# Second attention of a two-layer transformer on one core: the nine banks of max scores of a group in another order

## The chip, the cores and the metric

The kernel is one program on one core of a Trainium2 chip. The metric is the device time of one execution in microseconds (us). Five engines work side by side, each through its own list of instructions in order: PE (TensorE, matmuls; its weight loads are shown apart as PEld), DVE (VectorE), ACT (ScalarE), POOL (GpSimd) and SP (SyncE, which starts transfers). They wait for each other by semaphores.

## What is computed

Two layers: a linear attention and a mixture of experts, then a second attention with softmax and another mixture of experts. The change lies in the second attention alone. Cut to that:

```python
qkv = x @ Wqkv                                   # four sequences of 512, 32 query heads, 8 key heads
scores = jnp.einsum('bhqd,bhkd->bhqk', q, k) / math.sqrt(HD)
scores = jnp.where(causal, scores, -jnp.inf)
aw = jax.nn.softmax(scores, axis=-1)             # max over the keys, exp, sum
aw = aw[:, :, 0] - lam * aw[:, :, 1]
attn = jnp.einsum('bhqk,bhkd->bhqd', aw, v) * (1.0 - LAMBDA_INIT)
```

## The kernel before

The second attention (`phase_last`) runs over 32 groups (`GROUPS`), one for each sequence and key head. A group has 512 keys in four blocks of 128, and the queries of its four heads, 2048 rows in all, in 16 **granules** of 128 rows.

The softmax needs the maximum of each row before the exponential. So the scores are computed twice. The first time, `max_scores(g, a)` on PE (L1981 to L1998) computes the scores granule by granule; granule t has 32 x (t + 1) columns of keys, since the causal mask cuts the rest, so they run from 32 to 512 columns. The granules are packed into nine PSUM **banks** of at most 512 columns by the table `MAX_GRANULES` (L1219); entry a of the table says which granules are in bank a, and the physical bank is a modulo 3. On DVE, `maximum(g, a)` (L1709 to L1721) waits for the bank, adds the mask and reduces each granule of it to one column of `neg_max` (two rows in the trace for each: the reduction and the reading of its accumulator). Before PE may fill a bank again, DVE must be done with the bank three places earlier (`max_done`, L1990).

The second time, `scores(g, e)` (L2000) makes two matmuls of 512 columns for each of five steps e, a **score pair**, into two of four PSUM banks in turn; the maxima ride along as extra rows of the weights' operand. ACT takes the exponential of a pair in one instruction (`exponentials`, L1862 to L1869). Pair e may be written when the exponential of the pair two earlier is done. POOL cuts off the masked corner of the blocks on the diagonal, and `values(g, kb)` (L2013) multiplies the probabilities of key block kb with the values; its matmuls use a quarter of the array each.

The order on PE is written out by hand in the loop over the groups (L2122 on): while the scores of group g run, the maxima of group g + 3 (`LEAD`) are put between them, by `rows(...)`:

```python
scores(g, 0); rows(0); scores(g, 1); rows(1)
values(g - 1, 1), values(g - 1, 2), values(g - 1, 3)
rows(2); scores(g, 2); rows(3, 4); scores(g, 3); rows(5)
values(g, 0); rows(6); scores(g, 4); rows(7, 8)
```

`rows(n)` is place n of the table. This full pattern holds for groups 1 to 28. The maxima of groups 0 and 1 come before the loop, mixed with the last query, key and value products, those of groups 2 and 3 in group 0, two places for each call of `rows`, with short matmuls without use between them (`warming`). On DVE, `maximum` runs over all groups and places in the same order; in groups 0 and 1 the remainders of the queries (`remainders`, L1637), on which query products and later parts wait, come after the first four places. POOL splits the finished maxima of a group into three parts (`split_maxima`), and a transfer brings them to the place from which `scores` reads them, two groups later.

Of the kernel before, what the change touches and what calls it, by code (L numbers as in the profile page):

```python
# [1215 lines left out]
MASKED = -3.0e38  # L1216


MAX_GRANULES = [(15,), (14,), (13,), (12,), (11, 3), (10, 4), (9, 5), (8, 6), (7, 2, 1, 0)]  # L1219

SLOTS = [(kb, tq) for kb in range(NQ) for tq in range(kb, NQ)]
FIRST = [SLOTS.index((kb, kb)) for kb in range(NQ)]
NA, NE = len(MAX_GRANULES), len(SLOTS) // 2
NORM_AT = 2
# [5 lines left out]
def phase_last(nc, dram, sb, ps):  # L1230
# [3 lines left out]
    with ExitStack() as ctx:  # L1234
# [391 lines left out]
        def _(ve):  # L1626
# [82 lines left out]
            def maximum(g, a):  # L1709
# [4 lines left out]
                off = 0  # L1714
                for n, t in enumerate(MAX_GRANULES[a]):
                    width = 32 * (t + 1)
# [223 lines left out]
        def _(pe):  # L1940
# [40 lines left out]
            def max_scores(g, a):  # L1981
# [10 lines left out]
                off = 0  # L1992
                for t in MAX_GRANULES[a]:
                    width = 32 * (t + 1)
# [316 lines left out]
```

How the kernel before makes its waits and increments, by code:

```python
    def wait(self):  # L39
        self.eng.wait_ge(self.sem, self.base + self.n)
# [71 lines left out]
    def deviations(self, gp, b):  # L112
        gp.wait_ge(self.var_ready, b + 1)
        self.nc.gpsimd.tensor_tensor(self.rstd[:, b * NI:(b + 1) * NI], self.veps[:, b * NI:(b + 1) * NI],
                                     self.minus_half[:, 0:NI], ALU.pow).then_inc(self.rstd_ready, 1)
# [1 line left out]
    def lines(self, ve, b):  # L117
        ve.wait_ge(self.rstd_ready, b + 1)
        self.nc.vector.scalar_tensor_tensor(self.line[:, b * NI:(b + 1) * NI], self.mv[:, b * NI:(b + 1) * NI, 0], -1.0,
                                            self.rstd[:, b * NI:(b + 1) * NI], ALU.mult, ALU.mult).then_inc(self.line_ready, 1)
# [1 line left out]
    def normalise(self, ac, b):  # L122
        ac.wait_ge(self.line_ready, b + 1)
        for t in range(b * NI, (b + 1) * NI):
            last = self.nc.scalar.activation(self.xn[:, t, :], self.x[:, t, :], ACT.Identity, scale=self.rstd[:, t:t + 1],
                                             bias=self.line[:, t:t + 1])
        last.then_inc(self.xn_ready, 1)
# [74 lines left out]
    def choose(self, ve, ch, half):  # L202
# [1 line left out]
        def wide(ap):
            return ap.unsqueeze(2).to_broadcast([P, HALF, E])
        falling = self.sb["falling"][:].unsqueeze(1).to_broadcast([P, HALF, E])
        ve.wait_ge(self.logits_mm, 2 * half + 2)
        logits = self.ps[:, self.logits_bank[2 * half], 0:HALF * E].rearrange("p (t e) -> p t e", e=E)
        ch.link(nc.vector.tensor_reduce(self.top[:, t], logits, AX.X, ALU.max))
```

## Time and profile before

| | us |
|---|---|
| median of 3 runs | 586.7 |
| the runs | 586.08, 586.70, 589.87 |
| span of the profiled execution | 586.0 |
| PE matmul busy | 526.7 (90%) |
| PE weight load busy | 374.2 (64%) |
| DVE busy | 424.8 (72%) |
| ACT busy | 328.6 (56%) |
| POOL busy | 315.5 (54%) |

The span runs from the first to the last instruction of one profiled execution; its own time is about that of the fastest run, 586.08. Busy shares are means over stages with different limits: the stretch that this document speaks of reaches from about 165 us (the first max scores) to about 400 us (the last). All times in the rows are in microseconds from the span's start. PEclk is TensorE's granted clock as a share of 2.4 GHz. Matmuls are pipelined, so the ends of PE's rows are modelled and overlap with the next row's start; starts are what is compared.

### The profile page before, as it was taken

To read this page: it belongs to the slowest core of one execution; us is meant where nothing else is said; L and a number is where in the kernel's file an instruction comes from. 1 tells how busy PE (TensorE), PEld (TensorE's weight loads), DVE (VectorE), ACT (ScalarE), POOL (GpSimd) and SP (SyncE) were. 2 spreads that over 40 slices of the span, in tenths; PEclk is the share of its full clock that TensorE was granted. 3 is DMA by queue.
4 is the path that set the end of the run, shared out by engine and by line. 5 is a ranking of instruction groups with operands and counts; after the bars stand their busy time and mean duration, and the time that the engine had idled before them with its cause. 6 is when DMAs were issued, how large, how long until landed. Compare 5 with 4: busy or idle time off the path is not lost.

```text
span 586.0 us, 13132 instructions
## 1 busy us (share of the span) xinstructions
PE 526.7 (90%) x4044; PEld 374.2 (64%) x4044; DVE 424.8 (72%) x1662; ACT 328.6 (56%) x544; POOL 315.5 (54%) x478
## 2 busy tenths in 40 slices
PE   5989979967489999999999999999998899999960
PEld 5667769965157445444444454445577799999960
DVE  4776736735859899999999999996678454454436
ACT  3854426632573477777777777776630544444423
POOL 3441154417644486566686668666710677777630
PEclk9999989998699899999999999999999899999995
DMA  8500112221671546647634653433850111111115
GB/s 317 221 2 19 55 35 71 71 70 52 126 145 24 122 104 129 126 108 169 153 88 110 154 135 72 93 91 66 299 151 19 45 48 51 49 49 51 43 37 204
DMA packets 90498, 58.21 MB, mean 99 GB/s; under 512 B 72674, under 2 KB 76771, under 8 KB 88615
## 3 DMA queue, kind: packets, MB, share of 16 engines
q1 hardware_dynamic: 81550, 41.18, 28.0%
q0 software_dynamic: 3744, 7.68, 5.1%
q10 hardware_dynamic: 5136, 8.52, 4.1%
q8 instruction: 35, 0.57, 0.4%
q14 instruction: 33, 0.26, 0.2%
HBM read 37.72 MB, written 19.63 MB: 98 GB/s over the span
## 4 chain that ended last, share of the span: by engine, by line
PE 76%; DVE 12%; DMA 4%; issue 3%; ACT 3%; POOL 2%; SPq 0%; ACTq 0%; POOLq 0%; DVEq 0%
PE banks L1167 15%; PE banks L2021 13%; PE banks L2009 12%; PE banks L1995 11%; PE banks L1180 9%; DVE banks L1718 2%; PE banks L1961 1%; PE banks L1154 1%; PE banks L765 1%; DMA f_hg<-scratch_h_rows,r_source 1%; PE banks L366 1%; DMA a_at<-scratch_back_rows,home 1%; PE banks L2109 1%; DVE f_upd L1080 1%; DVE a_rest_ L1637 1%
## 5 line engine op out<-in xcount | busy, mean ns | idle before, releaser
L1718 DVE CUSTOM_DVE_ANT_1 banks<-banks,a_mask 128x480 f32<-128x480 f32 (+14 forms) x480 | 190.0, 459 | 14.7 <-PE banks L1995 12.9
L1867 ACT ACTIVATE a_prob_<-banks 128x1024 f32<-128x1024 f32 x160 | 154.1, 1021 | 48.7 <-PE banks L2009 48.7
L1534 POOL TENSOR_SCALAR_AFFINE_SELECT a_prob_<-a_prob_ 128x512 f32<-128x512 f32 x128 | 80.8, 635 | 67.0 <-ACT a_prob_ L1867 67.0
L1995 PEld LDWEIGHTS banks<-a_k_u_,a_q_u_ 72*128 72x128 bf16 x512 | 64.9, 148 | 64.5 <-DVE a_neg_max_ L1718 31.1
L1995 PE MATMUL banks<-a_k_u_,a_q_u_ 72*128 72x512 bf16 (+15 forms) x512 | 102.4, 291 | 2.4 <-DVE a_neg_max_ L1718 2.4
L1167 PE MATMUL banks<-f_hgt,f_w_now 128*112 128x128 f32 (+1 forms) x808 | 101.2, 277 | 0.0
L2009 PE MATMUL banks<-a_q_u_,a_k_x_ 75*128 75x512 bf16 x320 | 97.4, 386 | 0.4 <-ACT a_prob_ L1867 0.4
L1167 PEld LDWEIGHTS banks<-f_hgt,f_w_now 128*112 128x112 f32 (+1 forms) x808 | 95.6, 184 | 0.0
L978 POOL DMA_INDIRECT f_hg<-scratch_h_rows,r_source x62 | 59.6, 962 | 61.2 <-DVE r_source L299 31.6
L2021 PE MATMUL banks<-a_prob_,a_v_g_ 128*32 128x512 f32 (+3 forms) x1024 | 83.5, 444 | 0.4 <-POOL a_prob_ L1534 0.4
L1718 DVE DVE_READ_ACCUMULATOR2_ANT a_neg_max_<- 128x1 f32 x512 | 72.3, 143 | 0.0
L1180 PE MATMUL banks<-w,f_hidt 112*128 (+1 forms) x496 | 66.2, 277 | 0.0
L1180 PEld LDWEIGHTS banks<-w,f_hidt 112*128 112x128 f32 (+1 forms) x496 | 60.9, 193 | 0.4 <-issue 0.4
L1111 ACT COPY f_w_now<-w 128x448 f32 (+1 forms) x62 | 31.3, 506 | 41.8 <-issue 22.4
L984 POOL DMA_INDIRECT scratch_back_rows<-f_y,r_home x39 | 38.4, 984 | 27.3 <-DVE f_y L1056 26.9
L1042 DVE TENSOR_TENSOR f_hidt<-banks,f_sil 112x512 f32<-112x512 f32 x39 | 27.0, 692 | 33.6 <-PE banks L1167 28.0
L2021 PEld LDWEIGHTS banks<-a_prob_,a_v_g_ 128*32 128x32 f32 x1024 | 27.1, 110 | 37.0 <-issue 19.7
L1030 DVE COPY f_w_now<-w 128x448 f32 (+1 forms) x62 | 25.9, 418 | 30.7 <-issue 29.7
L1095 ACT COPY f_hgt<-banks 128x128 f32<-128x128 f32 x62 | 16.4, 265 | 52.2 <-PE banks L1154 52.2
L2009 PEld LDWEIGHTS banks<-a_q_u_,a_k_x_ 75*128 75x128 bf16 x320 | 26.6, 102 | 17.0 <-ACT a_prob_ L1867 12.5
L1512 POOL TENSOR_SCALAR a_k_x_<-a_k_u_ 72x512 bf16<-72x512 bf16 x32 | 35.4, 1105 | 0.1
L1878 ACT COPY a_o_sb_<-banks 128x512 f32<-128x512 f32 x32 | 18.7, 585 | 18.7 <-PE banks L2021 18.7
(247 smaller groups left out, 714.1 us busy)
## 6 DMA issues: line engine op xcount, KB each, us to landing
a_q_u_<-scratch_q_parts SPq DMA_DIRECT2D x15, 576.0 KB
scratch_o_rows<-a_o_sb_ ACTq DMA_DIRECT2D x28, 256.0 KB, 2.2
w<-in_w SPq DMA_DIRECT2D x2, 2048.0 KB, 10.5
w<-in_w SPq DMA_DIRECT2D x2, 1792.0 KB, 12.3
scratch_q_parts<-a_part_ SPq DMA_DIRECT2D x24, 128.0 KB
a_k_u_<-scratch_k_parts SPq DMA_DIRECT2D x48, 48.0 KB
f_back<-scratch_back_rows SPq DMA_DIRECT2D x4, 512.0 KB, 4.7
w<-in_w SPq DMA_DIRECT2D x2, 896.0 KB, 19.6
```

The source lines that it names most:

```text
L978: nc.gpsimd.indirect_dma_start(out=hg[s % AHEAD][:], out_offset=None, in_=h_rows[:, :], in_offset=bass.IndirectOffsetOnAxis(ap=source[:, s ...
L984: nc.gpsimd.indirect_dma_start(out=back_rows[:, :], out_offset=bass.IndirectOffsetOnAxis(ap=home[:, s:s + 1], axis=0), in_=y[s % YR][:], i ...
L1111: nc.scalar.copy(w_now[s % 2][:, 0, :], w_first(e)).then_inc(w_a, 1)
L1167: last = nc.tensor.matmul(PS[0:FC, 4 + 2 * q + n, c * P:(c + 1) * P], w_now[q][:, n, c * FC:(c + 1) * FC], hgt[q][:], start=True, stop=True)
L1180: last = nc.tensor.matmul(PS[:, 2 + q, 0:D], hidt[q][0:FC, c, :], w_down[0:FC, bass.ds(e, 1), c, :].rearrange("p a d -> p (a d)"), start=( ...
L1512: nc.gpsimd.tensor_scalar(k_x[g % RING][0:ROWS, :].rearrange("r (t c) -> r t c", c=CK), k_u[r][:, :, g % 2 * TG:(g % 2 + 1) * TG].rearrang ...
L1534: nc.gpsimd.affine_select(out=block_p, in_=block_p, pattern=[[0, JH], [1, P]], compare_op=ALU.is_ge, fill=0.0, base=0, channel_multiplier= ...
L1718: last = nc.vector.tensor_tensor_reduce(out=found, in0=found, in1=mask[:, :, TG - 4 * (t + 1):], scale=-1.0, scalar=-MASKED, op0=ALU.add, ...
L1867: nc.scalar.activation(prob[g % 2][:, 2 * e:2 * e + 2].rearrange("p s j t c -> p (s j) t c"), PS[:, b0:b0 + 2, :].rearrange("p s (j c t) - ...
L1995: last = nc.tensor.matmul(PS[:, a % 3, off:off + width], queries[:, g % 2, :, t], k_u[r][:, :, g % 2 * TG:g % 2 * TG + 4 * (t + 1)], start ...
L2009: last = nc.tensor.matmul(PS[:, 3 + 2 * ((NE * g + e) % 2) + n, :], k_x[g % RING][0:ROWS + PARTS, kb * P:(kb + 1) * P], queries[:, g % 2, ...
L2021: last = nc.tensor.matmul(PS[32 * j:32 * (j + 1), 7, kb * P:].rearrange("p (q f) -> p q f", f=P), v_g[g % VR][:, kb, :], prob[g % 2][:, FI ...
```

## The change

One line, the table that packs the granules into banks. The nine banks hold the same granules as before; the order in which they come is another. The bank of four small granules (256, 96, 64 and 32 columns, 448 in all; called the small bank below) moves from the last place to the first, the one of 384 and 128 columns to the second, and the others follow in a new order.

```diff
-MAX_GRANULES = [(15,), (14,), (13,), (12,), (11, 3), (10, 4), (9, 5), (8, 6), (7, 2, 1, 0)]
+MAX_GRANULES = [(7, 2, 1, 0), (11, 3), (15,), (14,), (8, 6), (9, 5), (13,), (12,), (10, 4)]
```

In columns, the places hold 512, 480, 448, 416, 512, 512, 512, 512, 448 before, and 448, 512, 512, 480, 512, 512, 448, 416, 512 after.

PE, in the loop, from the fifth score pair of a group to the first values of the next (L2009 are score pairs, L1995 max scores, L2021 values; `a_k_u`, `a_q_u` and `a_k_x` are keys and queries). Before:

```order
L2009 MATMUL banks<-a_q_u1_,a_k_x2_ 128x512 x2
L1995 MATMUL banks<-a_k_u2_,a_q_u2_ 128x288
L1995 MATMUL banks<-a_k_u2_,a_q_u2_ 128x224
L1995 MATMUL banks<-a_k_u2_,a_q_u2_ 128x256
L1995 MATMUL banks<-a_k_u2_,a_q_u2_ 128x96
L1995 MATMUL banks<-a_k_u2_,a_q_u2_ 128x64
L1995 MATMUL banks<-a_k_u2_,a_q_u2_ 128x32
L2009 MATMUL banks<-a_q_u1_,a_k_x3_ 128x512 x2
L1995 MATMUL banks<-a_k_u3_,a_q_u3_ 128x512
L2009 MATMUL banks<-a_q_u1_,a_k_x3_ 128x512 x2
L1995 MATMUL banks<-a_k_u3_,a_q_u3_ 128x480
```

The same place on PE after the change:

```order
L2009 MATMUL banks<-a_q_u1_,a_k_x2_ 128x512 x2
L1995 MATMUL banks<-a_k_u2_,a_q_u2_ 128x416
L1995 MATMUL banks<-a_k_u2_,a_q_u2_ 128x352
L1995 MATMUL banks<-a_k_u2_,a_q_u2_ 128x160
L2009 MATMUL banks<-a_q_u1_,a_k_x3_ 128x512 x2
L1995 MATMUL banks<-a_k_u3_,a_q_u3_ 128x256
L1995 MATMUL banks<-a_k_u3_,a_q_u3_ 128x96
L1995 MATMUL banks<-a_k_u3_,a_q_u3_ 128x64
L1995 MATMUL banks<-a_k_u3_,a_q_u3_ 128x32
L2009 MATMUL banks<-a_q_u1_,a_k_x3_ 128x512 x2
L1995 MATMUL banks<-a_k_u3_,a_q_u3_ 128x384
L1995 MATMUL banks<-a_k_u3_,a_q_u3_ 128x128
```

Between the fifth pair and the second pair of the next group stood 960 and 512 columns; now stand 928 and 448.

PE, from the end of the first value run to the next values, before:

```order
L2021 MATMUL banks<-a_prob0_,a_v_g1_ 32x128 x4
L1995 MATMUL banks<-a_k_u3_,a_q_u3_ 128x448
L2009 MATMUL banks<-a_q_u1_,a_k_x3_ 128x512 x2
L1995 MATMUL banks<-a_k_u3_,a_q_u3_ 128x416
L1995 MATMUL banks<-a_k_u3_,a_q_u3_ 128x384
L1995 MATMUL banks<-a_k_u3_,a_q_u3_ 128x128
L2009 MATMUL banks<-a_q_u1_,a_k_x3_ 128x512 x2
L1995 MATMUL banks<-a_k_u3_,a_q_u3_ 128x352
L1995 MATMUL banks<-a_k_u3_,a_q_u3_ 128x160
L2021 MATMUL banks<-a_prob1_,a_v_g2_ 32x512 x4
```

The same place on PE after the change:

```order
L2021 MATMUL banks<-a_prob0_,a_v_g1_ 32x128 x4
L1995 MATMUL banks<-a_k_u3_,a_q_u3_ 128x512
L2009 MATMUL banks<-a_q_u1_,a_k_x3_ 128x512 x2
L1995 MATMUL banks<-a_k_u3_,a_q_u3_ 128x480
L1995 MATMUL banks<-a_k_u3_,a_q_u3_ 128x288
L1995 MATMUL banks<-a_k_u3_,a_q_u3_ 128x224
L2009 MATMUL banks<-a_q_u1_,a_k_x3_ 128x512 x2
L1995 MATMUL banks<-a_k_u3_,a_q_u3_ 128x320
L1995 MATMUL banks<-a_k_u3_,a_q_u3_ 128x192
L2021 MATMUL banks<-a_prob1_,a_v_g2_ 32x512 x4
```

Directly behind the value run stands the bank of 512 columns instead of that of 448, and the two banks before the fourth pair have 992 columns instead of 928.

## Rows read from the trace of the kernel before

**Rows 1.** Busy time by stretch: us, PE, PEld, DVE, ACT, POOL, clock, DMA share, GB/s.

```profile
269.76:276.83 7.07, 7.07 (x62) 3.51 (x60) 6.72 (x35) 5.39 (x7) 4.97 (x10) 1.00 0.74 181
198.60:202.00 3.40, 3.40 (x27) 1.30 (x27) 1.83 (x11) 1.55 (x3) 2.48 (x6) 0.50 0.10 11
```

**Rows 2.** Who waited for whom, 225 to 390 us: total us, times, longest.

```profile
PEld banks L1995 <- DVE a_neg_max_ L1718: 21.2, 27, 0.8
```

**Rows 3.** PE's timeline of one group: start, us, instructions, [idle before <-releaser].

```profile
270.55 0.63 PE L2009 MATMUL banks<-a_q_u_,a_k_x_ 75*128 75x512 bf16 x2
271.03 0.36 PE L1995 MATMUL banks<-a_k_u_,a_q_u_ 72*128 72x480 bf16 x1
271.32 1.50 PE L2021 MATMUL banks<-a_prob_,a_v_g_ 128*32 128x384 f32 x24
272.76 0.41 PE L1995 MATMUL banks<-a_k_u_,a_q_u_ 72*128 72x448 bf16 x1
273.00 0.62 PE L2009 MATMUL banks<-a_q_u_,a_k_x_ 75*128 75x512 bf16 x2
273.46 0.56 PE L1995 MATMUL banks<-a_k_u_,a_q_u_ 72*128 72x416 bf16 x3
273.86 0.61 PE L2009 MATMUL banks<-a_q_u_,a_k_x_ 75*128 75x512 bf16 x2
274.31 0.38 PE L1995 MATMUL banks<-a_k_u_,a_q_u_ 72*128 72x352 bf16 x2
274.62 1.06 PE L2021 MATMUL banks<-a_prob_,a_v_g_ 128*32 128x512 f32 x8
275.61 0.45 PE L1995 MATMUL banks<-a_k_u_,a_q_u_ 72*128 72x320 bf16 x2
275.89 0.61 PE L2009 MATMUL banks<-a_q_u_,a_k_x_ 75*128 75x512 bf16 x2
276.35 0.64 PE L1995 MATMUL banks<-a_k_u_,a_q_u_ 72*128 72x288 bf16 x6
276.83 0.60 PE L2009 MATMUL banks<-a_q_u_,a_k_x_ 75*128 75x512 bf16 x2
277.27 0.38 PE L1995 MATMUL banks<-a_k_u_,a_q_u_ 72*128 72x512 bf16 x1
277.62 0.63 PE L2009 MATMUL banks<-a_q_u_,a_k_x_ 75*128 75x512 bf16 x2
```

**Rows 4.** The weight loader's timeline: after either value run, and before the second pair.

```profile
272.75 0.14 PEld L1995 LDWEIGHTS banks<-a_k_u_,a_q_u_ 72*128 72x128 bf16 x1 [0.20 <-issue]
...
275.61 0.21 PEld L1995 LDWEIGHTS banks<-a_k_u_,a_q_u_ 72*128 72x128 bf16 x2 [0.84 <-DVE a_neg_max_ L1718]
...
277.62 0.11 PEld L2009 LDWEIGHTS banks<-a_q_u_,a_k_x_ 75*128 75x128 bf16 x2 [0.42 <-ACT a_prob_ L1867]
```

**Rows 5.** The chain of waits: start, us, what (first and last of 26 such).

```profile
218.13 1.00 PE banks L2021 x8
...
394.86 1.00 PE banks L2021 x8
```

**Rows 6.** DVE's timeline: the small bank, the four banks behind it, one steady bank.

```profile
176.89 0.43 DVE L1718 CUSTOM_DVE_ANT_1 banks<-banks,a_mask 128x256 f32<-128x256 f32 x1 [1.42 <-PE banks L1995]
...
177.74 0.77 DVE L1718 CUSTOM_DVE_ANT_0 banks<-banks,a_mask 128x512 f32<-128x512 f32 x1
178.43 0.14 DVE L1718 DVE_READ_ACCUMULATOR2_ANT a_neg_max_<- 128x1 f32 x1
...
180.18 1.81 DVE L1637 TENSOR_TENSOR a_rest_<-banks,a_part_ 128x1024 f32<-128x1024 f32 x2
...
273.20 0.63 DVE L1718 CUSTOM_DVE_ANT_1 banks<-banks,a_mask 128x448 f32<-128x448 f32 x1 [0.28 <-PE banks L1995]
```

**Rows 7.** PE's timeline in group 0 and 1: a late bank and the first long value run.

```profile
196.67 0.47 PE L1995 MATMUL banks<-a_k_u_,a_q_u_ 72*128 72x256 bf16 x4 [0.32 <-DVE a_neg_max_ L1718]
...
198.56 2.79 PE L2021 MATMUL banks<-a_prob_,a_v_g_ 128*32 128x384 f32 x24
```

## The prediction

> **What bounds the kernel now.** The change lives in the second attention, so I read that stretch alone: first busy time by stretch, then the waits, then PE's own timeline of one group, and last the weight loader's timeline, to see which of the waits named there are real.
>
> Busy time by stretch shows one group of the steady part, 7.07 us long: PE busy for all of it, DVE for 6.72, ACT for 5.39, POOL for 4.97, at a granted clock of 1.00, which is 2.4 GHz [rows 1]. The chain of waits agrees: the first-block value product (the piece of 1.00 us) comes back from 218.13 to 394.86 us in 25 steps, 7.07 us each, nearly always by way of PE [rows 5]. Two engines are so close to full that the busy shares alone do not say which one sets the pace. The list of waits points at DVE: the weight loader waited for the maxima 27 times, 21.2 us in all [rows 2]. That is the reading to test.
>
> PE's timeline of a group [rows 3], by starts, runs from the second score pair at 270.55: score pair 0.48, bank of 480 columns 0.29, values 1.44, bank of 448 columns 0.24, pair 0.46, two banks with 928 columns 0.40, pair 0.45, bank of 512 columns 0.31, values 0.99, bank of 512 columns 0.28, and then at 275.89 the fifth pair 0.46, two banks with 960 columns 0.48, the next group's first pair 0.44, its first bank 0.35, and at 277.62 the second pair again. I call 270.55 to 275.89 the **rear piece** (5.34 us) and 275.89 to 277.62 the **front piece** (1.73 us). The 928 columns in 0.40 us give 0.43 ns a column. By this, 480 and 512 columns ahead of values carry a surcharge of 0.08 to 0.09 and the 448 and 512 behind values one of 0.05 to 0.06. Those surcharges are the change to and from the value product, not DVE: behind the first value run the weight loader's idle time is put down to "issue", behind the second to DVE (0.84 us), and both matmuls start equally soon [rows 4]. So the 21.2 us of waiting cost PE nothing in this stretch.
>
> One wait is real. The first bank of 512 columns takes 0.35 where 512 columns take 0.22: PE stands for about 0.13, because the weights of the second score pair wait 0.42 us for the exponential [rows 4]. That pair overwrites the two score banks that the fifth pair of the group before filled, and ACT has to read them first. The front piece is therefore set by a loop of score pair, exponential, score pair, whose length of 1.73 us does not depend on the banks of maxima inside it as long as they fit. PE's own work there is 0.46 + 0.48 + 0.44 + 0.22 = 1.60.
>
> **The change part by part.** Nothing is added or removed: 16 matmuls, 16 reductions and 4352 columns a group stay, and so do all the waits in the code. The banks move between the pieces.
>
> Front piece: seventh and eighth place of the table (counted from nought) and the next group's first. Before 960 + 512 columns; after 416 + 512 and the small bank of 448. The 928 columns cost 0.40. The small bank is not timed alone; the six matmuls with 960 columns took 0.48, of which 512 columns are 0.22, so it is 0.26 (bounds: 0.19 if its four matmuls cost only their columns, 0.48 as a whole group of six). PE's work becomes 0.46 + 0.40 + 0.44 + 0.26 = 1.56 (1.49 to 1.78), under 1.73. The piece stays at 1.73: the 0.04 us of work that left is only a longer wait for ACT, 0.17 instead of 0.13.
>
> Rear piece: places 1 to 6. Before 480 + 448 + 416 + 512 + 512 + 512 = 2880 columns; after 512 + 512 + 480 + 512 + 512 + 448 = 2976. The 96 more columns cost 0.04 us. The surcharges stay: one bank stands ahead of each value run and one behind it, as before. The number of matmuls ahead of the values goes from one to two, which costs nothing beyond columns in the rows (416, 384 and 128 follow one another at the plain column rate). So a group takes 7.11 in place of 7.07. The full pattern runs for groups 1 to 28: 28 x 0.041 = **+1.2 us**.
>
> DVE must not come late. A bank may be written when the one three places earlier is reduced. The narrowest place after the change is the sixth bank, which needs the third, now of 512 columns and directly behind the values. Before, a 448-column matmul at 272.76 [rows 3] had its reduction start at 273.20 [rows 6], 0.44 later; 64 more columns make 0.47. The reduction of 512 takes 0.69 (177.74 to 178.43) and its read-out 0.14 [rows 6]: done 1.30 after the third bank's matmul starts. PE comes to the sixth bank after 0.27 (bank) + 0.46 (pair) + 0.43 (992 columns) + 0.45 (pair) = 1.61, and to its weights one matmul of 0.22 sooner, 1.39. A margin of 0.09 on the weights and 0.31 on the matmul: no wait. DVE's own idle time moves: with the small bank and that of 384 and 128 first, it has less to do before the values end and waits longer for the third bank. That costs nothing, since PE does not wait for it.
>
> The stretch that fills the pipeline: groups 0 and 1 put their first four banks ahead of other work on DVE (the remainders of the queries, L1637). Those four took 180.18 − 177.74 = 2.44. After: the small bank 0.85 (176.89 to 177.74), 512 columns 0.69, 480 columns 0.65, and 384 with 128 at 0.69 plus one more granule (the small bank's three extra granules cost 0.85 − 448/512 x 0.69 = 0.25, so 0.08 each) 0.77: 2.96, all from [rows 6]. The remainders come 0.5 us later, but DVE is the bound there, its total is unchanged, and the banks that now follow are smaller by the same amount. Bounds: 0 and +0.5, if what PE starts behind the remainders is not caught up. I take 0, since the first value products behind it, at 198.56 [rows 7], come after all four groups of maxima.
>
> Sum: +1.2 us. The profiled execution's span is 586.0 and the fastest run 586.08, so about 0.1 lies around it: 587.3 by that execution. The median of the runs shown is 0.6 higher, 586.7: **587.9 us**.
>
> **The rivals.** (a) The change does nothing: PE's 0.35 at the first bank is its own cost and not a wait. Then the front piece gives back the 96 columns, 0.04, and the time stays 586.7. Against it: the same 512 columns take 0.22 elsewhere, and the weight loader's row names ACT.
>
> (b) DVE is the bound, faster. Then the 21.2 us of waits are real, and what counts is DVE's idle time of 0.35 a group (7.07 − 6.72). An order that fills it would save up to 28 x 0.35 = 9.8: 576.9. For it: the wait list, and 95% busy. Against it: the equal starts behind the two value runs. The Trainium skill (Perfetto Trace Analysis, Identifying the Most-Contended Engine) holds matmul busy time for a bad measure and asks for the share of weight loading; that is 3.51 of 7.07 here, half, and by this rule DVE would be called the fuller engine. The rows of starts speak against the rule in this stretch, since column time, surcharges and one wait fill the group.
>
> (c) DVE is late, slower. The third bank is ready 1.44 + 0.47 = 1.91 after the values start. If DVE at that start still has the whole last bank of the group before on hand (384-and-128-like, 0.77) and then the two first banks (0.85 + 0.77), it needs 2.39 and comes 0.48 late to the third; that is done 1.78 after its matmul, and PE, there at 1.61, waits 0.17 in each group: 28 x 0.17 = +4.8, with the +1.2 592.7. It decides from a backlog of some 0.6 at the start of the values. For it: DVE is 95% busy. Against it: the two banks just before are now of 416 and 512 columns instead of 512 and the small one, so less is on hand there than today.
>
> (d) The clock. From 198.60 to 202.00 the granted clock was 0.50, 1.2 GHz [rows 1], after PE had waited for DVE (0.32 us at 196.67), and the value run there took 2.79 us where it takes 1.50 [rows 7, 3]: 1.3 us, and some 0.3 for the bank and the pair behind it. PE's waits in the filling stretch move, above all that for DVE behind the remainders, which grows by the 0.5 us. One more such stretch: +1.6, 589.5. None: −1.6, 586.3. The Trainium skill (TensorE: Matmul & The Clock Gate, A second HAM failure mode) tells of short idle times between groups of matmuls that cycle through PSUM banks and bring the clock down. The steady group has such an idle time and a clock of 1.00, so the trace does not bear that out for the steady part.
>
> **How the numbers follow.** Forecast 0.68, (a) 0.12, (b) 0.04, (c) 0.03, (d) one more 0.08, none 0.05. The range leaves out (b) and (c), 0.07, and reaches from the lower clock case to the upper, with the 0.6 us by which runs lie off the median: 586.3 − 0.6 to 589.5 + 0.6, 585.7 to 590.1. It holds the bounds of the fill (+0.5) and of the small bank (at 0.48 the front piece would grow by 0.05 a group, +1.4: 589.3). A measurement of this kernel tells about 1% (5.9 us) from no change; only (b) lies below that and only (c) above: faster 0.04, within 1% 0.93, slower 0.03.
>
> **What would show it.** In the changed kernel's PE timeline a group should take 7.10 to 7.12 us by starts, the front piece 1.73, the rear piece 5.38, and the second score pair's weights should still wait for the exponential, a little longer. DVE should idle some 0.6 us in front of the third bank. The first value products behind the fill should start within 0.5 us of 198.56. A group of 7.07 speaks for (a), one under 7.0 for (b), a wait of PE for DVE at the sixth bank for (c), another count of stretches at 1.2 GHz between 160 and 210 us for (d). The forecast falls if the front piece changes its length with the banks in it.

## The result, and the profile after

The changed kernel takes 591.0 us in the median of 22 runs (586.77 to 595.89), the kernel before 587.13 us beside it (22 runs, 585.78 to 593.07). The ratio is 1.0067 (95% interval 1.0051 to 1.0083): 3.9 us slower, within 1%, but outside the range of 585.7 to 590.1. The forecast was +1.2.

The runs of one kernel lie in groups that go with the mean granted clock of the run; ratios leave out runs more than 1.5% above the fastest of their kernel, medians do not. For the changed kernel:

| mean clock of the run | runs | time, median | range |
|---|---|---|---|
| 0.960 to 0.961 | 2 | 587.7 | 586.8 to 588.6 |
| 0.958 to 0.959 | 13 | 590.6 | 589.8 to 592.1 |
| 0.947 to 0.951 | 7 | 594.6 | 593.3 to 595.9 |

The kernel before has 116 of its 121 runs in the batches below at 0.960 to 0.966. The profiled execution of the changed kernel took 586.77 us, one of the two in the first line, with a span of 584.9. So it shows what the change does at the high clock, and it does not show what makes most runs longer.

PE's timeline after the change, the small bank in the filling stretch and one steady group (start, us, instructions, idle before and releaser in brackets):

```profile
183.85 0.42 PE L1995 MATMUL banks<-a_k_u_,a_q_u_ 72*128 72x256 bf16 x4
184.12 0.47 PE L2035 MATMUL banks<-a_wqk,ident 128*128 128x128 f32 x2
...
269.46 0.62 PE L2009 MATMUL banks<-a_q_u_,a_k_x_ 75*128 75x512 bf16 x2
269.92 0.38 PE L1995 MATMUL banks<-a_k_u_,a_q_u_ 72*128 72x384 bf16 x2
...
273.27 0.38 PE L1995 MATMUL banks<-a_k_u_,a_q_u_ 72*128 72x320 bf16 x2
273.58 1.06 PE L2021 MATMUL banks<-a_prob_,a_v_g_ 128*32 128x512 f32 x8
274.58 0.41 PE L1995 MATMUL banks<-a_k_u_,a_q_u_ 72*128 72x448 bf16 x1
274.82 0.62 PE L2009 MATMUL banks<-a_q_u_,a_k_x_ 75*128 75x512 bf16 x2
275.29 0.56 PE L1995 MATMUL banks<-a_k_u_,a_q_u_ 72*128 72x416 bf16 x3
275.68 0.61 PE L2009 MATMUL banks<-a_q_u_,a_k_x_ 75*128 75x512 bf16 x2
276.13 0.42 PE L1995 MATMUL banks<-a_k_u_,a_q_u_ 72*128 72x256 bf16 x4
276.56 0.62 PE L2009 MATMUL banks<-a_q_u_,a_k_x_ 75*128 75x512 bf16 x2
```

Against [rows 3]: the rear piece runs from 269.46 to 274.82, 5.36 us (5.34 before), the front piece from 274.82 to 276.56, 1.74 us (1.73 before), the group 7.10 (7.07). Over all steady groups the median from group to group is 7.099 against 7.065. The small bank, the last before 276.56, takes 0.43 there; in the filling stretch, at 183.85, the same bank of another group takes 0.27. The difference of 0.16 is a wait inside the front piece. (The rows left out are the first value run, the third to fifth bank and two pairs.)

The list of waits of the steady part, from 225 to 388 us (us in all, times, longest):

```profile
PEld banks L1995 <- DVE a_neg_max_ L1718: 22.6, 39, 0.8
...
DVE banks L1718 <- PE banks L1995: 9.2, 20, 0.5
```

The weight loader still waits some 22 us for the maxima, as in [rows 2], and DVE now idles for a bank, at most 0.5 us at a time. Neither moves a start on PE.

What else changed for PE lies in the filling stretch, in PE's timeline behind the remainders of the queries. After the change:

```profile
179.78 0.59 PE L2035 MATMUL banks<-a_wqk,ident 128*128 128x256 f32 x2
181.89 0.40 PE L1995 MATMUL banks<-a_k_u_,a_q_u_ 72*128 72x416 bf16 x1 [1.51 <-DVE a_neg_max_ L1718]
```

Before, the same wait, ahead of the same place of the table, was 1.27 us long:

```profile
182.82 0.44 PE L1995 MATMUL banks<-a_k_u_,a_q_u_ 72*128 72x288 bf16 x2 [1.27 <-DVE a_neg_max_ L1718]
```

In both executions the clock stayed at 1.00 over it.

### The profile page after: what moved, and what is told of

Its sections match the earlier page's. It is cut to its first block, busy times and chain, and to the rows that moved or that the text cites. A ratio compares the mean times of both kernels' runs of the same rounds, so it can differ in the third digit from the quotient of the medians.

```text
span 584.9 us, 13132 instructions
## 1 busy us (share of the span) xinstructions
PE 526.5 (90%) x4044; PEld 380.1 (65%) x4044; DVE 424.3 (73%) x1662; ACT 328.5 (56%) x544; POOL 316.0 (54%) x478
## 4 chain that ended last, share of the span: by engine, by line
PE 76%; DVE 11%; DMA 4%; POOL 3%; ACT 3%; issue 3%; SPq 0%; ACTq 0%; POOLq 0%; DVEq 0%
PE banks L1167 16%; PE banks L2021 13%; PE banks L2009 12%; PE banks L1995 11%; PE banks L1180 9%; DVE banks L1718 2%; POOL a_at L1559 2%; PE banks L1961 1%; PE banks L1154 1%; PE banks L765 1%; PE banks L366 1%; DMA f_back<-scratch_back_rows 1%; DMA f_hg<-scratch_h_rows,r_source 1%; PE banks L2109 1%; DVE a_rest_ L1637 1%
## 5 line engine op out<-in xcount | busy, mean ns | idle before, releaser
L1718 DVE CUSTOM_DVE_ANT_1 banks<-banks,a_mask 128x256 f32<-128x256 f32 (+14 forms) x480 | 187.8, 461 | 6.8 <-PE banks L1995 6.8
L1995 PEld LDWEIGHTS banks<-a_k_u_,a_q_u_ 72*128 72x128 bf16 x512 | 69.4, 147 | 69.3 <-DVE a_neg_max_ L1718 33.9
L1995 PE MATMUL banks<-a_k_u_,a_q_u_ 72*128 72x256 bf16 (+15 forms) x512 | 102.5, 291 | 2.8 <-DVE a_neg_max_ L1718 2.6
L2009 PE MATMUL banks<-a_q_u_,a_k_x_ 75*128 75x512 bf16 x320 | 98.0, 388 | 0.7 <-ACT a_prob_ L1867 0.5
L2021 PE MATMUL banks<-a_prob_,a_v_g_ 128*32 128x512 f32 (+3 forms) x1024 | 83.2, 443 | 0.3 <-POOL a_prob_ L1534 0.3
L2021 PEld LDWEIGHTS banks<-a_prob_,a_v_g_ 128*32 128x32 f32 x1024 | 27.0, 110 | 31.3 <-issue 19.6
L2009 PEld LDWEIGHTS banks<-a_q_u_,a_k_x_ 75*128 75x128 bf16 x320 | 29.4, 102 | 11.7 <-ACT a_prob_ L1867 1.7
L1718 DVE CUSTOM_DVE_ANT_0 banks<-banks,a_mask 128x512 f32<-128x512 f32 x32 | 22.4, 700 | 12.8 <-PE banks L1995 12.8
```

What stands on the lines that cost most here:

```text
L1718: last = nc.vector.tensor_tensor_reduce(out=found, in0=found, in1=mask[:, :, TG - 4 * (t + 1):], scale=-1.0, scalar=-MASKED, op0=ALU.add, ...
L1995: last = nc.tensor.matmul(PS[:, a % 3, off:off + width], queries[:, g % 2, :, t], k_u[r][:, :, g % 2 * TG:g % 2 * TG + 4 * (t + 1)], start ...
L2009: last = nc.tensor.matmul(PS[:, 3 + 2 * ((NE * g + e) % 2) + n, :], k_x[g % RING][0:ROWS + PARTS, kb * P:(kb + 1) * P], queries[:, g % 2, ...
L2021: last = nc.tensor.matmul(PS[32 * j:32 * (j + 1), 7, kb * P:].rearrange("p (q f) -> p q f", f=P), v_g[g % VR][:, kb, :], prob[g % 2][:, FI ...
```

## The experiments

The theory formed from this: the steady part costs +1.0 as forecast, and the other 2.9 us are stretches in which PE runs at 1.2 GHz in place of 2.4, brought on by the longer wait in the fill and by the tail's new place in time. (The tail is all that follows the last value products at about 422 us: projections, the router and the second mixture of experts.) The rival: DVE, reordered, is late in the steady part of the longer runs (c).

**The same two kernels again.**

> The changed kernel once more, for a profile of an execution that takes the time most of its runs take (591.0 us; the profile in hand is of one at 586.8). Theory A, the clock: the group stays at 7.10 us by PE's starts, and the execution shows one to three more stretches at a granted clock of 0.5 than the one in hand, about 1.6 us each. Theory B, the steady part: a group takes 7.16 us or more (+3.9 over 28 groups), with a wait of PE for DVE at the sixth bank. Ratio to the kernel before about 1.007 by either.

> The kernel before as it is, for its clock and span run by run and a second profile. Ratio 1.000 within 0.002. Theory A: its usual mean clock lies above that of the changed kernel by what two or three stretches at half clock make (0.003 to 0.009). Theory B: the same mean clock within 0.001.

In this batch the kernel before took 586.78 (29 runs). The changed kernel gave 592.48 (6 runs, 587.4 to 597.51), ratio 1.0087 (1.0057 to 1.0118); the kernel before as a copy 587.18, ratio 1.001 (0.9999 to 1.0021), with all twelve runs at a clock of 0.961 to 0.964. So the loss belongs to the change; and the changed kernel again had clocks from 0.944 to 0.963. Its profile fell once more on a run of the short kind (587.4 us, group 7.10), so it could not decide between A and B.

**The new order in the filling stretch alone, and in the steady part alone.** The groups whose maxima are made before the loop or in its first pass (0 to 3) have one table, all others the other:

```diff
+def granules(g, a):
+    return (NEW_GRANULES if g < 4 else MAX_GRANULES)[a]     # fill_new; steady_new: g >= 4
-                for t in MAX_GRANULES[a]:
+                for t in granules(g, a):
```

> The new order of banks in groups 0 to 3 alone (the maxima before and in the first pass of the loop), the old one from group 4 on. Theory A (waits in the filling stretch bring the clock down): +2.5 to +3 us, ratio about 1.005, and a lower clock. Theory B (steady part): 0, ratio 1.000.

> The old order in groups 0 to 3, the new one from group 4 on. Theory A: +1.0 us (28 groups less none of the fill, 34 ns each by the changed kernel's profile), ratio 1.002, the clock of the kernel before. Theory B: +3.9 us, ratio about 1.007. If both this and the other half give under 1 us, the cause lies in where the two orders meet or in the phase of the clock's stretches against the program.

`fill_new` splits into two kinds of run: five at 585.9 to 588.3 us with a clock of 0.960 to 0.966, and seven at 594.1 to 599.5 with 0.939 to 0.950. The ratio is 1.0045 (1.0009 to 1.0082); the median of all twelve is 594.17, 7.4 above before where 2.5 to 3 were expected. Its profiled execution is the longest of the second kind (599.5 us). Its busy time by stretch (us, PE, PEld, DVE, ACT, POOL, clock, DMA share, GB/s), and then PE's timeline behind the remainders:

```profile
180.00:185.00 5.00, 3.48 (x13) 1.83 (x12) 4.67 (x18) 1.56 (x2) 1.13 (x2) 0.81 0.01 2
185.00:200.00 15.00, 15.00 (x62) 10.10 (x60) 10.03 (x46) 4.10 (x4) 4.38 (x11) 0.50 0.46 105
200.00:204.00 4.00, 3.29 (x18) 1.74 (x15) 3.39 (x15) 1.13 (x2) 0.64 (x1) 0.93 0.00 0
```

```profile
182.07 0.40 PE L2001 MATMUL banks<-a_k_u_,a_q_u_ 72*128 72x416 bf16 x1 [1.52 <-DVE a_neg_max_ L1724]
182.31 0.60 PE L2041 MATMUL banks<-a_wqk,ident 128*128 128x256 f32 x2
182.83 0.45 PE L2001 MATMUL banks<-a_k_u_,a_q_u_ 72*128 72x352 bf16 x2
183.11 1.11 PE L2041 MATMUL banks<-a_wqk,ident 128*128 128x256 f32 x2
```

PE waits 1.52 us, works for one microsecond at full speed, and from 183.1 on the same pair of matmuls takes 1.11 in place of 0.60. The clock is 0.50 throughout 185 to 200 us, PE is busy 15.00 of 15.00, and DVE only 10.03: at half clock PE is the bound of this stretch. A second stretch at half clock follows from 203.6, 17.1 us long too. In the profiled execution of the changed kernel, where the clock fell only at 196.5, DVE is nearly as full as PE:

```profile
185.00:200.00 15.00, 14.14 (x93) 8.50 (x95) 14.03 (x74) 6.21 (x7) 7.01 (x18) 0.89 0.47 105
```

`steady_new` took 589.63, ratio 1.004 (1.0022 to 1.0059), and also has two kinds: five runs at 586.7 to 588.9 (clock 0.960 to 0.963, median 587.7) and seven at 589.5 to 591.0 (0.958, median 590.7). The first kind is 0.9 above before, the +1.0 of the steady part. The second has 3.0 us more. So neither theory's figure came (A +1.0, B +3.9): there are two kinds of run here as well. Its profiled execution is of the second kind, and its group is 7.10 us as in the changed kernel's of 586.77 us, so (c) falls: nothing in the steady part is late. The tail is different. Stretches of `steady_new`:

```profile
425.00:430.00 5.00, 5.00 (x26) 4.24 (x26) 3.74 (x17) 0.73 (x2) 0.00 (x0) 0.66 0.94 216
456.00:464.00 8.00, 6.45 (x32) 6.19 (x33) 1.83 (x4) 4.15 (x8) 5.06 (x6) 0.57 0.15 43
```

and of the changed kernel's execution of 586.77 us:

```profile
425.00:430.00 5.00, 4.67 (x33) 3.71 (x33) 3.72 (x17) 1.17 (x2) 0.00 (x0) 1.00 0.93 213
456.00:464.00 8.00, 7.41 (x56) 7.40 (x56) 2.52 (x5) 4.96 (x10) 4.67 (x6) 0.79 0.16 42
```

Two stretches at half clock have been added, one from 425.8 (3.4 us) and one that makes the stretch at 456 6.8 us long in place of 3.4. Both executions stood at the same place to 0.02 us when the first one fell, as PE's timelines show, `steady_new` first, and only there the matmuls at 425.6 take 1.85 in place of 1.09:

```profile
423.81 1.85 PE L366 MATMUL banks<-router,a_at 128*128 128x8 f32 x16
425.59 1.85 PE L2095 MATMUL banks<-ident,a_late_a 128*64 128x128 f32 x8
```

```profile
423.79 1.85 PE L366 MATMUL banks<-router,a_at 128*128 128x8 f32 x16
425.57 1.09 PE L2089 MATMUL banks<-ident,a_late_a 128*64 128x128 f32 x8
```

The two programs are alike from group 4 on. So the work of the program alone does not decide the clock; its place against something that the program does not start with seems to do so too. The Trainium skill (TensorE: Matmul & The Clock Gate, Part 1: The HAM clock gate) says that the watch over PE's activity runs freely and does not restart with a kernel; these two pairs of rows agree with that.

**The wait in the fill, taken away and lengthened.** The loop that makes group 1's maxima has one useless pair of matmuls behind each bank to keep PE busy (`warming`). `fill_warm` is `fill_new` with three more pairs where PE waits; `less_warm` is the kernel before without the pair there. Nobody reads what these pairs compute.

```diff
-                warming(7, 1, 256)
+                warming(7, 4 if a == 6 else 1, 256)         # fill_warm
+                if a != 6: warming(7, 1, 256)               # less_warm
```

> The new order in groups 0 to 3 alone, and three more matmuls of 256 columns without use on PE behind place 6 of group 1, where PE waits 1.5 us for DVE. Theory A1 (that wait brings the clock down for some 17 us in part of the runs): no run near 594 any more, median 586.5 to 587.0, mean clock 0.963 to 0.966 in every run. Theory B1 (the order itself, by DVE or by the later score pairs, makes the slow runs): still about half of the runs at 594, as in fill_new.

> The old order everywhere, but without the matmul without use behind place 6 of group 1, so that PE stands there for 1.7 us instead of 1.3 at an unchanged order. It leaves out no part of the computation. Theory A1: runs near 594 with a mean clock of 0.945 to 0.951 appear, in a third of the runs or more. Theory B1: 586.8 in all.

PE's row at this place in `fill_warm`:

```profile
182.06 1.89 PE L2041 MATMUL banks<-a_wqk,ident 128*128 128x256 f32 x8
184.18 0.40 PE L2001 MATMUL banks<-a_k_u_,a_q_u_ 72*128 72x416 bf16 x1 [0.23 <-DVE a_neg_max_ L1724]
```

With the wait at 0.23 us, the runs of 594 us and more are gone: 587.9 us (586.5 to 587.0 expected), ratio 0.9997 (0.9978 to 1.0017), eleven of twelve runs at 0.960 to 0.966 and the twelfth at 0.955 (590.06). In `less_warm`, which has the old order, the wait is longer than after the change:

```profile
182.07 0.44 PE L1995 MATMUL banks<-a_k_u_,a_q_u_ 72*128 72x288 bf16 x2 [1.73 <-DVE a_neg_max_ L1718]
```

and its stretches show the clock fall at this place (from 183.9, 6.8 us long):

```profile
180.00:185.00 5.00, 3.27 (x18) 2.14 (x17) 5.00 (x25) 2.01 (x3) 1.52 (x2) 0.89 0.01 2
185.00:200.00 15.00, 14.30 (x77) 9.52 (x76) 13.03 (x63) 5.47 (x6) 5.13 (x13) 0.81 0.46 105
```

It took 591.95, ratio 1.0054 (1.0022 to 1.0086), against 587.32 before; nine of eleven runs have a clock of 0.946 to 0.955. Its profile has the two stretches of the tail besides. So the new order of the banks is not needed for the loss. Taking a clock under 0.957 for the sign of a fall in the fill (only `fill_new` and `less_warm` have a profile with one), it falls the oftener the longer this one wait is: in one run of 24 at 0.22 to 0.23 us (with `after_warm`, below), three of the 34 of the kernel before at 1.27, a third to somewhat over half at 1.51 (7 of 22, 3 of 6, 7 of 12), nine of eleven at 1.73.

**The tail's place in time, moved without the change.** `pad4` computes the third score pair of groups 27 and 28 twice in the kernel before, `pad15` 15 such matmuls in groups 21 to 28. PE has 0.9 and 3.4 us more work.

```diff
+                twice = (2 if g in (27, 28) else 0) if e == 2 else 0                       # pad4
+                twice = (2 if 21 <= g <= 27 else 1 if g == 28 else 0) if e == 2 else 0     # pad15
-                for n, (kb, tq) in enumerate(SLOTS[2 * e:2 * e + 2]):
+                for n, (kb, tq) in pair[:twice] + pair:
```

> The old order everywhere; in groups 27 and 28 the third score pair is computed twice, four more matmuls, which make all that follows 0.9 us later. Theory A2 (the phase of what follows against the stretches at half clock decides on two of them behind 420 us): +2.5 to +3.2 us in most runs, clock 0.958. Theory B2 (the steady part alone is longer, and the rest of steady_new's loss comes from the new order in the steady part): +0.9, clock 0.964.

> As pad4, but 15 more matmuls over groups 21 to 28, 3.4 us, about the length of one stretch at half clock as the profiles show it (3.41). Theory A2 (phase): the tail meets the clock as in the kernel before, +3.4 us and clock 0.963 to 0.964, so not much more than pad4 for nearly four times the work. Theory C2 (anything later loses two more stretches): +5.5 us, clock 0.958. Theory B2: +3.4, clock 0.964 here, and +0.9 for pad4.

Before took 587.32. `pad4`: 590.21, ratio 1.0037 (1.0017 to 1.0057), eight of twelve runs at a clock of 0.958, and in its profile the two stretches of `steady_new`:

```profile
425.00:430.00 5.00, 5.00 (x29) 4.39 (x29) 3.88 (x18) 0.58 (x1) 1.01 (x2) 0.67 1.02 214
456.00:464.00 8.00, 5.53 (x25) 5.27 (x26) 2.72 (x8) 4.12 (x8) 5.52 (x7) 0.59 0.19 50
```

`pad15`: 590.40, ratio 1.005 (1.0031 to 1.0069), no run at 0.958, and the clock of the kernel before:

```profile
425.00:430.00 5.00, 4.83 (x37) 4.07 (x37) 2.98 (x14) 1.49 (x3) 1.89 (x2) 1.00 1.00 217
456.00:464.00 8.00, 5.49 (x33) 5.34 (x34) 2.42 (x7) 4.32 (x9) 5.68 (x6) 0.79 0.18 50
```

By the medians 0.9 us of work costs 2.9, and 3.4 us of work costs 3.1 (by the ratios 2.2 and 2.9, each within 1.2). So a microsecond of delay ahead of the tail is enough to bring the two stretches in most runs, whether the new order makes it or other work, and a delay of the length of one stretch does not bring them.

The traces say more. Eleven of the profiled executions have the stretch at half clock that in [rows 1] starts at 198.60, and the tail unaltered ahead of the late features; the time from the start of that stretch to the router's first product sorts them:

| profiled execution | from the early stretch to the router, us | clock fell between 424 and 427 us |
|---|---|---|
| kernel before (two), `before_const`, `fill_warm` | 225.66 to 225.75 | no |
| `pad4`, `steady_new`, `after_warm_const` | 226.74 to 226.80 | yes |
| changed kernel (two), `after_warm` | 226.93 to 227.25 | no |
| `pad15` | 229.32 | no |

The changed kernel lies at 227.25 in one execution and at 226.93 in the other: one program meets the clock's stretches at different places from run to run. That the 13 runs at 0.958 lay nearer 226.8 would fit, but was not measured.

**Mending the changed kernel.** `after_warm` is the changed kernel with the four pairs in the fill. `after_warm_tail` puts useless matmuls (`constants`) ahead of the late features' transposes and between the router's products as well. `after_warm_const` has the four pairs and six more useless matmuls in the wait for the experts' first rows:

```diff
-            constants(6, 1)
+            constants(6, 2)               # after_warm_tail, with one more constants(6, 1) between the logits
-            constants(4, 4)
+            constants(4, 10)              # after_warm_const
```

> The changed kernel with three more matmuls of 256 columns without use behind place 6 of group 1, where PE waits for DVE. By the two-part reading (a low clock in the filling stretch in a third of the runs, and two more stretches at half clock behind 420 us in most others): the runs at 593 to 596 with a clock of 0.947 to 0.951 go, those at 590 to 591 with 0.958 stay, median 590.0 to 590.5. If the whole loss came from the filling stretch: 588.0.

> As after_warm, and two more blocks of one 256-column matmul without use behind the last values, around the 16 matmuls of 8 columns of the router (L366) in which the profiles with clock 0.958 show the stretch at half clock from 426 us. Cost on PE if nothing else changes 0.9 us. If too little work for PE there brings the clock down: clock 0.963 to 0.964 and 588.5 to 589. If the clock there does not follow PE's work: 591, clock 0.958.

> The changed kernel with the fill's wait covered (as after_warm) and with ten instead of four matmuls without use in PE's wait for the first rows of the experts (as before_const). If the late stretches at half clock hang on that wait (456 to 463 us in the profiles with clock 0.958): no stretch at half clock between 450 and 470 us, mean clock 0.965 to 0.967, median 587.0, 0.2 to 0.5 us above the kernel before, no runs over 589. If they hang on the router's small matmuls at 424 us alone: five of twelve runs stay at 589 to 591.

`after_warm`: 588.19 against 586.78, ratio 1.003 (1.0011 to 1.0049), no run under 0.958. It was expected at 590.0 to 590.5; five of twelve runs have the clock of 0.958 (median 590.2), where the changed kernel has it in 13 of the 15 runs that did not fall in the fill. That the tail is hit less often with the fill mended was not foreseen and stays open. `after_warm_tail`: 589.45, ratio 1.004 (1.0025 to 1.0056), 0.958 in two runs only, but 1.3 us more than `after_warm`: the added work is not paid back. `after_warm_const`: 587.83 against 587.67 (23 runs, one of them, of 1056 us, unexplained), ratio 1.0012 (0.9995 to 1.003). Expected were no runs over 589; five of twelve lie at 589.2 to 590.1, at clocks of 0.960 to 0.963, and none of these was profiled. Its profiled execution (586.98) has the stretch at 425 and not that at 456:

```profile
425.00:430.00 5.00, 4.76 (x23) 3.77 (x22) 3.52 (x16) 1.17 (x2) 0.00 (x0) 0.67 0.85 193
456.00:464.00 8.00, 6.74 (x55) 6.23 (x56) 2.67 (x6) 4.71 (x10) 5.22 (x6) 1.00 0.17 49
```

so in this execution the two come apart: the one follows the router's small products, the other stood behind the wait for the experts' rows, which is now filled.

**The kernel before, without its own stretches.** `before_const` has the six matmuls, `before_twice` computes the fifth score pair of group 0 twice (at the stretch of [rows 1], 198.60), `before_const_twice` does both.

> The kernel before with ten instead of four matmuls without use behind the router's slots (L2109), in the 3.05 us in which PE waits for the first rows of the experts; a stretch at half clock stands behind it in every profile (458 to 461 us). If that wait brings it: 1.5 us faster, ratio 0.9975, clock 0.968 to 0.970. If not: 0, or up to +0.5 if the matmuls end behind the rows.

> The kernel before with the fifth score pair of group 0 computed twice (0.45 us of PE's work where PE waits 1.1 us for DVE in the next two microseconds). If those waits bring the stretch at half clock from 198.6 us: 1.6 us faster, ratio 0.997, clock 0.968 to 0.970. If it stays: 0 to +0.4.

> The kernel before with both additions: the fifth score pair of group 0 twice and ten matmuls behind the router's slots. before_twice took away the stretch at half clock at 198.6 us and got one more at 453.6 us; with the wait there covered that one should go too: 584.3 to 585.0, ratio 0.996 to 0.997, clock 0.970 or more. If stretches at half clock only move on: 586, clock 0.967.

The kernel before has in these stretches:

```profile
196.00:202.00 6.00, 5.68 (x38) 2.29 (x39) 4.43 (x25) 2.64 (x4) 3.11 (x7) 0.72 0.25 40
453.00:461.00 8.00, 4.56 (x25) 4.00 (x24) 2.13 (x9) 3.80 (x7) 5.87 (x7) 0.81 0.16 42
456.00:464.00 8.00, 7.05 (x47) 6.89 (x48) 2.44 (x5) 4.50 (x9) 4.61 (x5) 0.79 0.19 49
```

`before_const`: 585.96 against 586.78, ratio 0.9987 (0.9971 to 1.0003). The stretch at 458 is gone, and the wait for the experts' rows (3.05 us in PE's timeline before) is 0.31. Expected was −1.5, measured −0.8, with no change still inside the interval. `before_twice`: 586.33, ratio 1.0 (0.9983 to 1.0017), where 1.6 us were expected. Its stretches:

```profile
196.00:202.00 6.00, 6.00 (x53) 2.64 (x52) 5.90 (x31) 4.46 (x5) 3.49 (x9) 1.00 0.35 73
...
453.00:461.00 8.00, 6.78 (x34) 6.52 (x35) 1.52 (x3) 4.30 (x8) 4.80 (x6) 0.57 0.17 49
```

The stretch in the fill is gone (1.00 where the kernel before has 0.72 from 196 to 202), but everything behind it comes sooner, and the late stretch has grown from 3.4 to 6.8 us (0.57 where before has 0.81 from 453 to 461). With both, neither is there:

```profile
196.00:202.00 6.00, 5.66 (x50) 2.89 (x54) 5.89 (x29) 4.18 (x6) 3.16 (x8) 1.00 0.26 52
...
453.00:461.00 8.00, 6.80 (x50) 5.78 (x48) 3.13 (x7) 4.33 (x9) 5.66 (x6) 1.00 0.20 53
```

`before_const_twice` takes 584.42 against 587.67, ratio 0.9958 (0.9941 to 0.9975): it beats the kernel before, and so the changed one. By the medians that is −3.3 where the two alone gave −0.8 and −0.5; by the ratios −2.5 against −0.8 and 0.0, each within 1.0, so that it is more than both together is at the edge of what the runs can tell.

## Why the prediction was wrong, step by step

**Right: the steady group.** Rear piece 5.36 (5.38 forecast), front piece 1.74 (1.73), group 7.10, and 28 x 0.034 = +1.0 where +1.2 stood. The front piece did not change with the banks in it, as a loop of score pair, exponential, score pair would have it. The small bank takes 0.27 by itself, as estimated (0.26), and 0.16 of waiting stands in the front piece, as forecast (0.17). The weight loader's row no longer names ACT for it, so of the sign that was named, the longer wait there, the trace shows only the time and not the releaser. DVE idles up to 0.5 for a bank (0.6 forecast for the third), and there is no wait at the sixth bank. With that (a), (b) and (c) fall for the steady part.

**Failed: "I take 0" for the fill.** The time on DVE was right: the first four banks take 2.96 us there after the change (176.28 to 179.24), as worked out, and the remainders come 0.5 later. PE's wait behind them grew, from 1.27 to 1.51. The working asked only whether that time is caught up by the first value products. Those are not at 198.56, as it says, but earlier:

```profile
193.00 1.06 PE L2021 MATMUL banks<-a_prob_,a_v_g_ 128*32 128x512 f32 x8
```

and after the change

```profile
191.72 1.06 PE L2021 MATMUL banks<-a_prob_,a_v_g_ 128*32 128x512 f32 x8
...
196.48 0.99 PE L2009 MATMUL banks<-a_q_u_,a_k_x_ 75*128 75x512 bf16 x2
```

From the first max scores (166.43 and 164.96) they are 26.56 and 26.76 us away: +0.2, between the bounds of 0 and +0.5. The long value run of [rows 7] is no measure of it, though it comes 0.7 later: in the changed kernel's execution the clock fell at 196.5, ahead of that run at 197.83 (the pair at 196.48 takes 0.79 to the next start in place of 0.44), in the kernel before's only as the run began. From the first max scores to the last value product the two executions differ by +0.9 (256.44 and 257.36), in the second pair of profiles by +1.05, so the forecast of +1.2 is nearly met at the high clock. What the working did not ask is what PE's longer wait does to the clock: it put that at nothing in the sum. In the profile of `fill_new` the clock falls one microsecond behind the wait and stays at 1.2 GHz for 17 us, and 7 of 22 runs of the changed kernel have times (593.3 to 595.9) and clocks (0.947 to 0.951) like those runs of `fill_new`.

**Failed: the price and the chance of (d).** It named the right wait, "that for DVE behind the remainders", and priced one more stretch at 1.6 us with a chance of 0.08. Measured, the fall in the fill costs some 8.0 us (medians of 594.8 and 586.8 for the two kinds of run within `fill_new`). The one such execution that was profiled has two stretches of 17.1 us, five times the length that was priced, and took 599.5; that the runs at 594.8 have one of them is an estimate from their mean clock, which at 0.946 to 0.950 over 593 us makes some 17 to 22 us more at half clock than 0.964 over 585 (twice the share that lacks to 1, times the span). And the two stretches in the tail were not looked for at all: the rival's sign was confined to 160 to 210 us, though the trace of before has stretches at half clock at 458 and 570 too. Going by the clock of `steady_new`'s profile, 0.958, they come in 13 of 22 runs, and cost some 2.9 us (590.6 against 587.7; 3.0 within `steady_new`). The median of the changed kernel lies among these runs: 587.1 + 1.0 + 2.9 = 591.0.

**Small: the time around the span.** The fastest run and the profile's span were set side by side as if they were one execution, 0.1 us apart. The profiled execution of after has both: 586.77 and 584.9, 1.9 apart. The execution of before with a span of 586.0 took about 587.9. This did not touch the difference that was forecast, nor the 587.9, which was built on the median.

**Open.** What sets where a run meets the clock's stretches cannot be told from the program. In the fill no order like that of the tail shows: from the stretch at half clock near 149 us to the end of PE's wait, `fill_new`, whose clock fell, has 33.08 us, and the changed kernel, whose clock did not, 33.13 and 32.72. No profile was taken of an execution of the changed kernel itself with the clock down; what happens in those is read from `fill_new` and `steady_new`, which hold its two parts.

## What to carry to other kernels

A change that costs nothing because the engine it touches waits anyway may still lengthen a wait of PE elsewhere, and the price can then be the clock's, as here: look at the longest waits of PE in the whole kernel, what the granted clock does behind them, and in how many runs. Before a loss of a few us is explained by the code that was changed, delay the same place by useless work of the same length, and of another: where 0.9 us cost 2.9 and 3.4 us cost 3.1, it is the place in time that costs. A few matmuls without use in the waits ahead of half-clock stretches were cheap here, but clear of noise (−2.5 us by the ratio) only when they stood at both such places at once.

## What the hardware showed that was not expected

- Once the clock had fallen behind the wait of 1.52 us, it stayed at 0.50 for 17.1 us while PE was busy 15.00 of 15.00 us, and was back at 0.93 in the mean from 200 to 204. Full work of PE did not bring it back soon.
- Most stretches at half clock in the profiles last 3.4, 6.8, 10.2 or 17.1 us, the shortest or a multiple of it. Two programs alike from group 4 on, at the same point to 0.02 us from the span's start, had one at 425.8 in one execution and none in the other; from the early stretch they were 226.75 and 227.25 us away.
- Taking one stretch away early brought a longer one late (`before_twice`: 3.4 us gone at 198.6, 6.8 in place of 3.4 at 453.6), so in these profiles stretches do not add up like terms of a sum.
